# Retention in a three-layer kernel: value weights centred per head once instead of the heads at every tile, heads copied out of PSUM by ACT, and the group norm's 2-column operations reading PSUM

## What is computed

```python
x = x + retention(group_norm(x))            # 32 groups of 8 channels, over all tokens
# retention, per image, 8 heads of 32:
q, k, vr = xf @ Wq.T, xf @ Wk.T * SCALING, xf @ Wv.T
qr, kr = theta_shift(q, sin, cos), theta_shift(k, sin, cos)
qk = einsum('bhqd,bhkd->bhqk', qr, kr) * mask
den = clip(abs(qk).sum(-1), 1, 50000)
out = einsum('bhqk,bhkd->bhqd', qk / den, vr)
out = (out - out.mean(-1)) / sqrt(out.var(-1) + 1e-5) * ln_g + ln_b   # over the 32 of a head
out = gelu(out) @ Wo.T
```

## Time and profile before

| | us |
|---|---|
| median of three runs | 2511.39 (2510.68 to 2511.53) |
| profiled execution, its time | 2514.61 |
| its span, first to last instruction | 2512.8 |
| busy: PE, DVE, ACT, POOL | 2375.8, 1823.9, 1463.7, 1054.7 |
| retention, first to last step (38 to 1065 of the span): PE, DVE, ACT, POOL | 914.89, 787.22, 683.20, 814.31 of 1027 |

### The profile page before, as it was taken

One profiled execution on the slowest core, in us unless ns is written; L12 is line 12 of the kernel. 1 busy time (PEld: TensorE's weight loads), 2 busy tenths in 40 slices (PEclk: granted clock), 3 DMA queues, 4 the chain that ended last, 5 costly groups with the idle time before them and its releaser, 6 DMA issues.

```text
span 2512.8 us, 38637 instructions
## 1 busy us (share of the span) xinstructions
PE 2375.8 (95%) x14870; PEld 1623.9 (65%) x14870; DVE 1823.9 (73%) x2766; ACT 1463.7 (58%) x2077; POOL 1054.7 (42%) x766
## 2 busy tenths in 40 slices
PE   8898989898989899899999999999999999999999
PEld 3333334343434343499898878888888888888887
DVE  6777777777777777767777757667776777767775
ACT  4666666666667676655565545545555555555554
POOL 4787878787878788522432302111100011111110
PEclk9999999999999999999999989999999999999999
DMA  6333434343434344416355340000000000000000
GB/s 238 85 77 80 106 75 107 66 108 74 104 70 107 76 101 98 101 59 95 73 91 90 68 110 26 26 26 26 26 26 26 26 18 18 18 25 26 26 26 17
DMA packets 89270, 165.73 MB, mean 66 GB/s; under 512 B 21488, under 2 KB 62840, under 8 KB 80768
## 3 DMA queue, kind: packets, MB, share of 16 engines
q1 hardware_dynamic: 80016, 97.21, 14.4%
q0 software_dynamic: 9072, 66.06, 13.1%
HBM read 71.93 MB, written 25.26 MB: 39 GB/s over the span
## 4 chain that ended last, share of the span: by engine, by line
PE 86%; DVE 7%; issue 4%; ACT 1%; POOL 1%; another core or an unknown queue 0%; DVEq 0%; ACTq 0%; POOLq 0%
PE scores L1755 9%; PE scores L1756 9%; PE scores L1757 9%; PE scores L429 9%; PE pairC L442 8%; PE pairD L358 5%; DVE l_prod L572 4%; PE pairC L461 3%; PE pairD L367 3%; PE pairC L1755 2%; PE pairC L1756 2%; PE pairC L1757 2%; PE pairD L1755 2%; PE pairD L1756 2%; PE pairD L1757 2%
## 5 line engine op out<-in xcount | busy, mean ns | idle before, releaser
L572 DVE TENSOR_TENSOR l_prod<-scores,l_window 128x1024 f32<-128x1024 f32 x512 | 602.7, 1219 | 179.3 <-PE scores L429 176.4
L770 ACT ACTIVATE l_absp<-l_prod 128x1024 f32<-128x1024 f32 x512 | 527.7, 1052 | 218.1 <-DVE l_prod L572 163.7
L2145 POOL TENSOR_TENSOR e_xnorm<-e_res,e_scale 128x1024 f32<-128x1024 f32 x16 | 39.0, 2440 | 775.2 <-DMA e_res<-t2T_scratch 775.2
L1914 ACT ACTIVATE e_r<-scores,e_bn,e_rs 128x512 f32<-128x512 f32 x256 | 197.9, 779 | 273.3 <-PE scores L1757 273.2
L891 POOL TENSOR_TENSOR l_absp<-l_absp,l_absp 128x1024 f32<-128x1024 f32 x126 | 297.2, 2381 | 19.0 <-ACT l_absp L770 19.0
L2021 DVE CAST e_h1hi<-e_r 128x512 fp32r<-128x512 f32 x256 | 147.1, 575 | 206.4 <-ACT e_r L1914 206.2
L442 PE MATMUL pairC<-l_prod,l_v 128*32 128x512 f32 x2048 | 279.3, 618 | 0.0
L1924 ACT ACTIVATE e_r<-scores,e_bn,e_rs 128x512 f32<-128x512 f32 x250 | 194.9, 781 | 136.9 <-PE scores L1757 135.6
L429 PEld LDWEIGHTS scores<-l_qhi,l_khi 32*128 32x128 f32 x1024 | 50.0, 184 | 310.2 <-DVE l_prod L572 236.4
L2048 DVE TENSOR_TENSOR e_r<-e_r,e_wbc 128x512 f32<-128x512 f32 x250 | 170.9, 691 | 85.5 <-ACT e_r L1924 85.2
L2023 DVE TENSOR_TENSOR e_h1lo<-e_r,e_h1hi 128x512 fp32r<-128x512 f32 x256 | 208.4, 814 | 8.8
(11 more groups left out here) (264 smaller groups left out, 5282.2 us busy)
## 6 DMA issues: line engine op xcount, KB each, us to landing
l_absp<-l_absp POOLq DMA_DIRECT2D x63, 1024.0 KB, 7.0
l_xo<-in_x SPq DMA_DIRECT2D x32, 256.0 KB, 2.6
x_scratch<-l_xo SPq DMA_DIRECT2D x32, 256.0 KB, 2.5
l_xa<-x_scratch SPq DMA_DIRECT2D x8, 1024.0 KB, 8.1
l_xr<-x_scratch SPq DMA_DIRECT2D x8, 1024.0 KB, 5.3
t2T_scratch<-l_xt SPq DMA_DIRECT2D x8, 1024.0 KB, 14.4
e_scale<-rows_scratch SPq DMA_DIRECT2D x16, 512.0 KB, 4.1
e_res<-t2T_scratch SPq DMA_DIRECT2D x16, 512.0 KB, 5.0
```

Of the source, the lines that this page charges most:

```text
L572: nc.vector.tensor_tensor(prod[2 * (S % 2) + j][:], sc[j][:], win[:, 4 * g + 2 * j:4 * g + 2 * j + 2, w0:w0 + QC], ALU.mult).then_inc(prod ...
L770: nc.scalar.activation(absp[S % ABS][j][:], prod[2 * (S % 2) + j][:], ACT.Abs).then_inc(abs_ready, 1)
L1914: nc.scalar.activation(r1[:, m, :], p1[m], ACT.Relu, bias=bn_[0][1][:, m, n:n + 1], scale=rs[0][:, m, n:n + 1]).then_inc(r1_ready, 1)
```

## The change

What it does, in `layer0`:

- `head_sums` and `centre` are gone from every phase. In their place DVE centres the value weights `wv` once in the start-up (`value_sums`, `centre_values`), and PE's first value projection waits for that.
- ACT's `squares` reads the transposed heads in `pB`; a new ACT copy, `take_heads`, puts them into `tA` as the last instruction of kt 2. POOL's scaling and PE's next user of `pB` wait for it (`heads_taken`).
- `group_mean` no longer has `gmean`; its differences and the square are read from and written to columns 2 to 5 of the bank `pA`, so that every one of its operations has at most one input in SBUF. It moves from behind kt 5 to behind `products` of kt 4, ahead of the shuffle of k. The second average and `group_var` move from kt 5 and kt 6 to kt 7, and the value projection in these phases from kt 6 to kt 5, as in the others. POOL's `group_rstd` moves behind the rotation of k. The sums of the group-norm phases stand where they do in the others.

```diff
-        if has_gn(P):
-            return ((5, (0, 1)), (7, (2, 3)), (7, (4, 5)), (9, (6, 7)))
...
-        a_tasks += [("gn1", P), ("gn2", P)] if has_gn(P) else []
+        a_tasks += [("gn1", P)] if has_gn(P) else []
         a_tasks += [("v", P)] if has_kv(P) else []
+        a_tasks += [("gn2", P)] if has_gn(P) else []
...
-                pe.wait_ge(centred if before[0] == "nT" else z_ready, before[1] + 1)
+                pe.wait_ge(heads_taken if before[0] == "nT" else z_ready, before[1] + 1)
...
+        pe.wait_ge(wv_centred, 1)
         project_v(0, 0, (0, 1), num, first_made)
...
-            if kt == 5 and part == 1 and has_gn(P):
+            if kt == 7 and part == 1 and has_gn(P):
                 a_free(("gn2", P))
                 group_sums(gvar[:], gvar_ready, b + 2)
             if kt == 5 and len(outs(P)) == 2:
                 out_proj(*outs(P)[1], (part,))
-            if kt == (6 if has_gn(P) else 5) and has_kv(P):
+            if kt == 5 and has_kv(P):
                 if part == 0:
...
-        nT = pB[:].rearrange("p (m d) -> p m d", d=32)
-
-        def head_sums(P):
-
-            dve.wait_ge(b_ready, b_order["nT", P] + 1)
-            nc.vector.tensor_reduce(nsum[:], nT, AX.X, ALU.add).then_inc(nsum_ready, 1)
-
-        def centre(P):
-
-            dve.wait_ge(nsum_ready, P + 1)
-            nc.vector.scalar_tensor_tensor(tA[:].rearrange("p t (h d) -> p (t h) d", d=32),
-                                           nsum[:].unsqueeze(2).to_broadcast([128, 16, 32]), -1.0 / HD, nT,
-                                           ALU.mult, ALU.add).then_inc(centred, 1)
+        wv_heads = wv[:].rearrange("p k (h d) -> p (k h) d", d=32)
+
+        def value_sums():
+
+            dve.wait_ge(weights_in, 16 * NWEIGHTS)
+            nc.vector.tensor_reduce(nsum[:], wv_heads, AX.X, ALU.add).then_inc(wv_sums, 1)
+
+        def centre_values():
+
+            dve.wait_ge(wv_sums, 1)
+            nc.vector.scalar_tensor_tensor(wv_heads, nsum[:].unsqueeze(2).to_broadcast([128, 16, 32]), -1.0 / HD, wv_heads,
+                                           ALU.mult, ALU.add).then_inc(wv_centred, 1)
...
         def group_mean(b, a):
             dve.wait_ge(a_ready, a + 1)
             nc.vector.tensor_scalar(gneg[:], pA[:, 0:2], -1.0, None, ALU.mult).then_inc(gneg_ready, 1)
-            nc.vector.tensor_copy(gmean[:], pA[:, 0:2]).then_inc(gmean_ready, 1)
-            dve.wait_ge(gmean_ready, 3 * b + 1)
-            nc.vector.tensor_tensor(dmean[:], mv[:, :, 0], gmean[:], ALU.subtract).then_inc(gmean_ready, 1)
+            nc.vector.tensor_tensor(dmean[:], mv[:, :, 0], pA[:, 0:2], ALU.subtract).then_inc(gmean_ready, 1)
+            nc.vector.tensor_tensor(pA[:, 2:4], mv[:, :, 0], pA[:, 0:2], ALU.subtract).then_inc(gmean_ready, 1)
             dve.wait_ge(gmean_ready, 3 * b + 2)
-            nc.vector.tensor_tensor(dmean[:], dmean[:], dmean[:], ALU.mult).then_inc(gmean_ready, 1)
+            nc.vector.tensor_tensor(pA[:, 4:6], dmean[:], pA[:, 2:4], ALU.mult).then_inc(gmean_ready, 1)
             dve.wait_ge(gmean_ready, 3 * b + 3)
-            nc.vector.tensor_tensor(gvar[:], mv[:, :, 1], dmean[:], ALU.add).then_inc(gvar_ready, 1)
+            nc.vector.tensor_tensor(gvar[:], mv[:, :, 1], pA[:, 4:6], ALU.add).then_inc(gvar_ready, 1)
 
         def group_var(b, a):
...
+        value_sums()
         first_normalise()
+        centre_values()
...
-            if kt == 1 and P > 0:
-                head_sums(P - 1)
-            if kt == 2 and P > 0:
-                centre(P - 1)
             if kt == 3 and P > 0:
                 clip_den(P - 1)
                 variance(P - 1)
+            if kt == 4 and has_gn(P):
+                group_mean(b + 1, a_order["gn1", P])
             if kt == 4 and has_kv(P):
                 shuffle(prep_k(P))
             if kt == 5 and outs(P):
                 add_residual(*outs(P)[0])
             if kt == 6 and len(outs(P)) == 2:
                 add_residual(*outs(P)[1])
-            if kt == 5 and has_gn(P):
-                group_mean(b + 1, a_order["gn1", P])
-            if kt == 6 and has_gn(P):
+            if kt == 7 and has_gn(P):
                 group_var(b + 1, a_order["gn2", P])
...
-            act.wait_ge(centred, P + 1)
-            nc.scalar.activation(sq[:], tA[:], ACT.Square, scale=HD ** -0.5).then_inc(sq_ready, 1)
+            act.wait_ge(b_ready, b_order["nT", P] + 1)
+            nc.scalar.activation(sq[:].rearrange("p t c -> p (t c)"), pB[:], ACT.Square, scale=HD ** -0.5).then_inc(sq_ready, 1)
+
+        def take_heads(P):
+            nc.scalar.activation(tA[:].rearrange("p t c -> p (t c)"), pB[:], ACT.Copy).then_inc(heads_taken, 1)
...
-            if kt == (7 if has_gn(P) else 6) and has_kv(P):
+            if kt == 6 and has_kv(P):
                 v_take(a_order["v", P], (P // 2 + 1) % 2, P % 2)
...
                 high(prep_q(P))
+            if kt == 2 and P > 0:
+                take_heads(P - 1)
...
+            pool.wait_ge(heads_taken, P + 1)
             tv = tA[:].rearrange("p t (h d) -> p (t h) d", d=32)
             nc.gpsimd.tensor_tensor(tv, tv, fac[:].unsqueeze(2).to_broadcast([128, 16, 32]),
                                     ALU.mult).then_inc(on_ready, 1)
...
             pair(P, 4)
-            if has_gn(P):
-                group_rstd(P // 4 + 1)
             if has_kv(P):
                 rotate(prep_k(P), P % 2)
                 rotated(prep_k(P))
+            if has_gn(P):
+                group_rstd(P // 4 + 1)
```

More of the change, by code:

```diff
@@ L197, in layer0 @@
     stats, mv = sb("stats", [128, 2, 2, 6]), sb("mv", [128, 2, 2])
-    gmean, dmean, gvar, grstd = (sb(n, [128, 2]) for n in ("gmean", "dmean", "gvar", "grstd"))
+    dmean, gvar, grstd = (sb(n, [128, 2]) for n in ("dmean", "gvar", "grstd"))
     mhalf = sb("mhalf", [128, 16])
@@ L337, in a_free @@
             elif before[0] == "gn1":
-                pe.wait_ge(gmean_ready, 3 * (before[1] // 4 + 1) + 1)
+                pe.wait_ge(gvar_ready, before[1] // 4 + 2)
             elif before[0] == "gn2":
@@ L644, in first_normalise @@
             dve.wait_ge(grstd_ready, 1)
+            dve.wait_ge(gneg_ready, 1)
             for c in range(2):
                 for k in range(2):
-                    nc.vector.tensor_scalar(xn[:, k, QC * c:QC * c + QC], raw[:, k, QC * c:QC * c + QC], gmean[:, k:k + 1],
-                                            grstd[:, k:k + 1], ALU.subtract, ALU.mult).then_inc(first_xn, 1)
+                    nc.vector.tensor_scalar(xn[:, k, QC * c:QC * c + QC], raw[:, k, QC * c:QC * c + QC], gneg[:, k:k + 1],
+                                            grstd[:, k:k + 1], ALU.add, ALU.mult).then_inc(first_xn, 1)
         def first_shuffle(n):
@@ L723, in tail @@
         def tail(point):
-            if point == 0:
-                head_sums(last)
-                centre(last)
             if point == 1:
@@ L851, in tail @@
                 squares(last)
+                take_heads(last)
             if point == 6:
@@ L1152, in early_tensor @@
         if left == 1 and kt == 4 and part == 0:
-            pe.wait_ge(a.r.centred, a.r.PHASES - 1)
+            pe.wait_ge(a.r.heads_taken, a.r.PHASES - 1)
             head_transposes(1)
```

6 lines of the change are left out of this document (3 added, 3 removed).

## The result

The changed kernel takes 2467.61 us (median of three runs, 2465.38 to 2469.18) against 2511.39: a ratio of 0.9826, 95% interval 0.9803 to 0.9848. Predicted were 2466.4. Its profiled execution is the one of 2467.61 us, with a span of 2465.8.

The account below looks back on a forecast made before the run. PE held 86% of the chain of waits; kt 2 and the group norm were overlong. 41.7 + 3.4 - 0.4 + 2.0 - 1.7 = 45.0 off 2511.4 gave 2466.4 us; range 2452 to 2480, 8 in 10 2444 to 2484.

Parts of the forecast that it names:

- the new wait: At scores 5 to 6, waiting for ACT's take of k: 1.01 of the 1.18 us saved at kt 2 lost.
- The regular phases: Phases 4 to 29 without the seven with the norm: 20 x 0.17 = 3.4 us less.
- the step behind the norm: Scores 0 to 1 after a norm phase, 4.45 us against 4.20: 1.7 us more over seven.
- the norm phases: Seven phases with the group norm at 31.27 us each, 218.9 against 260.63: 41.7 us less.
- the last two phases: They take no k at kt 4, so keep 1.0 of 1.18 us each: 2.0 us less.
- phases 2 and 3: Without output projection, the new wait makes scores 6 of each 0.2 us later: 0.4 us lost.
- the start-up and phase 0: Centring the weights in the start-up falls into existing waits: 0 us; uncovered, 1.4 once. Phase 0 had no term.
- Clock 1.00 in norm phases: Sign of being right: the seven norm phases at about 31.3 us with PE's granted clock at 1.00.
- ACT not holding the ring: Rival, chance 0.12: POOL's rotation or ACT's queue comes out earlier than read; 29 us more gained, 2437 us.
- Slower through POOL: Rival, chance 0.05: POOL delays the high part of q, over 7.7 us behind scores 2; 2517 us at 1.8 late.
- The small operations wait for POOL all the same: Rival, chance 0.08: two waits of 2.3 us stay, at kt 4 ahead of kt 5's products; 32 us less gained, 2498.

Follow-up runs that it names:

- the heads' part alone: Number 3: the kernel before with centred value weights, the copy on ACT, no head work on DVE, group norm untouched: 2499.83 us, ratio 0.9953.
- numbers 5 and 6: On the changed kernel: ACT's copy of the heads ahead of the high part of q, 2449.77 us; a second copy ahead of the real one, 2480.54 us.
- number 2: The changed kernel with the group norm's small operations put back to SBUF operands, at the new place: 2465.32 us.

## Why the prediction was right, and where it was not

The total: retention's last scores start 45.0 us earlier in the profiled execution (1007.48 against 1052.45), and the sum was 45.0. The mechanism was right: the small operations no longer wait for POOL, and ACT's take of k is the new wait. That the total fits to the tenth is luck. The regular phases gave 5.2 more than their term and the step behind the norm 1.7 more; the norm phases gave 0.6 less, the last two phases 1.1 less, phases 2 and 3 3.1 less, and the start-up and phase 0 took 2.2 that had no term. Low clock in four steps (kt 1 of phase 0, kt 6 of phases 1 and 3, kt 5 of phase 30) costs the changed kernel's profile 8.3 us more than the profile before; without it the sum would have been too small by about that.

**The norm phases.** Predicted 31.27 at a clock of 1.00 and 41.7 for the seven. Measured 31.00 in six, 33.47 in phase 1, and 260.63 - 219.49 = 41.1. The steps are right one by one: the take of k 18.76 us into phase 9 (predicted 18.77), no small operation above 0.17. Scores 6 came 0.27 earlier than predicted (23.51 into the phase for 23.78).

**The regular phases.** The term was 20 x 0.17 = 3.4 and measured 8.6, 0.43 each. The mechanism was right, the take at 18.73; the size was wrong by one reading. I took the products of kt 5 to start 1.59 behind the take because they did so before. But there they started 1.02 behind scores 5 (335.20 against 334.18), which is just what products do when they wait for their scores: 1.59 was not the length of take and shuffle, only an upper bound. In phase 7 after the change it is 270.02 - 268.63 = 1.39. With it the working gives 0.37. The same 0.2 is most of what the norm phases came out shorter.

**Clock.** "Clock 1.00 in norm phases" failed in phase 1, and phase 3 has such a step as well. I had reasoned from PE's idle of 1.2 us at kt 2; in the phases without an output projection the new wait leaves it idle 2.6 to 2.8 us. Phases 2 and 3 together are 3.5 us longer, where -0.4 stood as a loss; 2.8 of it is the low clock of one step. Start-up and phase 0 are 2.2 us longer (retention starts at 28.01 for 27.10; kt 1 of phase 0 takes 6.72 for 5.45). The first is not the price of centring: the heads' part alone has the same start-up work and starts at 26.89.

**Last two phases and the step behind the norm.** 0.9 of the 2.0 came, and again the low clock took the rest: kt 5 of phase 30 took 7.23 us for 5.55, and without it these phases would have given 2.6. The step from scores 0 to 1 is 345.19 - 340.96 = 4.23 for 4.45 predicted, 4.20 before: the 1.7 us was not spent.

**Rivals.** ACT not holding the ring is refuted by numbers 5 and 6. Slower through POOL didn't come: the high part of q starts 7.66 behind scores 2 in phase 9, as before (324.86 - 317.20, and 329.98 - 322.32). "The small operations wait for POOL all the same" was priced at 2 x 2.3 us a phase at kt 4; number 2 shows that this price was wrong whatever the cause, since SBUF operands don't wait at kt 4 either. The working never asked what POOL would be doing at the new place. The Trainium skill ("SBUF — State Buffer", Who interferes with whom) says that two SBUF inputs contend with a POOL operation that reads SBUF; the traces agree for POOL's scaling of 512 columns and its additions of 1024 (number 3: 1.03 and 2.26 us), and not for its power on 16, which by its inputs is such an operation and held up nothing (number 2: 0.16 to 0.19 beside 2.92); there the measurement decides. The price that the Trainium skill ("VectorE: DVE Perf Modes", the section on the TRN2 errata) puts on a PSUM source, 2.3 us in all by the prediction's estimate from its figures, isn't seen: 0.15 to 0.17 us from PSUM here, 0.16 to 0.19 from SBUF in number 2.

**The range.** The text puts its bounds for 8 in 10, 2444 and 2484, halfway to the two rivals at 2437 and 2498. Halfway from the forecast would be 2452 and 2482; only the lower one is halfway from the edge of the forecast's own range. The result lies inside either way.

**What the forecast missed in worth.** It took the change as one. Apart, the PSUM operands give all of it, the heads' part 10.8 more, and the new place of the norm gives 13 back by the medians (56.1 against 43.0). Between the profiled executions it is 9.9: 6.5 in six norm phases, and 2.5 in phases 1 to 3 and 1.7 in phase 30, mostly steps at low clock. The new place stands in a stretch that the take of k had just made critical.
